# A three-block sequence mixer on one Trainium2 core: parts of VectorE's work handed to ScalarE, GpSimd and TensorE, taps interleaved, and a new hop list

## The chip, the core and the metric

The kernel runs on one NeuronCore of one Trainium2 chip. The metric is the device time of one execution in microseconds (us), as the median of several runs. Engine names as in the profile: PE is TensorE (PEld its weight loads), DVE is VectorE, ACT is ScalarE, POOL is GpSimd, SP is SyncE, whose queue issues all DMAs here.

## The reference, cut to what matters

The input x is 16 batches of 256 tokens with 128 channels, all float32. Four residual blocks follow one another, each on a layer norm of x: a log-linear state-space attention (32 heads of 64), a transformer layer with 16-head attention and 8 experts (top 2), a gated mix of nine shifted copies, and the transformer layer again with the same weights.

```
xBC = sum(xp[:, i:i+T, :] * conv_w[:, i] for i in range(4));  xBC = silu(xBC)      # taps, edge, silu
x, Bm, Cm = split(xBC);  dt, lam = softplus(...), softplus(...)                      # gates
qk = einsum('btgn,bsgn->bgts', Cm, Bm)                                               # qk
att = qk * decay * lam_ts                                                            # weigh, wexp, prod
y = einsum('bhts,bshp->bthp', att, v) + x * D                                        # own, sum
out = x + (y * silu(z) normalised) @ out_proj_w.T + out_proj_b                       # gated, ssq, outp
probs = softmax(q k^T * scale);  out = probs @ v                                     # es, exps, ep, tail 0
h = relu(x @ W1[e] + b1[e]);  ff += w[e] * (h @ W2[e] + b2[e])                       # up, relu, down, acc
```

## The kernel before, in words

The work of one batch is cut into some 290 small steps called hops (`gates` 0 to 6, `conv`/`tap`/`taps`/`silu`/`xt`/`xcopy` 0 to 8, `weigh`/`wexp`/`prod`/`own`/`sum`/`gated` 0 to 7, `smax`/`rowmax`, `es`/`exps`/`ep`, `tail`, `up`/`relu`/`down`/`acc` 0 to 7, `mix` and so on). The string PERIOD is the list of all hops in one turn, written out by hand or by a planner, and "+2" behind a hop means that it works on the batch of two turns ago. `order()` repeats the list for 16 batches plus the largest lag, so in the middle of the run every turn does one whole batch of work, spread over parts of five batches. Each engine walks the same list in order and does its own part of each hop. An engine therefore never overtakes: a wait in one hop holds all its later hops.

The eight PSUM banks form two rings of four (psA for the state-space block, psB for the rest), handed out in list order. PE may run ahead of the engines that empty the banks only by these four.

The parts that the change touches, with the lines of the profile:

- `taps` (L1132): the causal convolution of two channel tiles, three multiply-adds each on DVE from PSUM. Each add waits for the one before it on the same tile, and one tile is done after the other. L1141 then corrects the first three columns of both tiles (the edge), which releases `silu` on ACT (L888).
- `qk` (PE L589, DVE L1145 to L1156): three 128x128 products of B and C. DVE copies them to SBUF, multiplies two of them with the identity and sums rows to get the diagonal, and makes `ccoef`, for which `own` on POOL (L1433) waits.
- `prod` (DVE L1164): the product of the decay weights with QK, for each of eight units one 128x1024 tile on the diagonal, and for the last four units another one off the diagonal, so 12 per batch.
- `gates` 3 and 4 (DVE L1060, L1062, L1065, L1070): pieces of softplus on 128x640.
- `ep` (DVE L1223): copies the attention's sums from PSUM, eight of 128x256 per batch.
- `tail` 0 (DVE L1232, L1234): reciprocal and scaling for each half of the tokens in turn.
- Setup on POOL (L1349 to L1365): fills of the level buffers, q_stack, k_stack and V9, all ahead of batch 0's `gates` 6 (L1370 to L1376), whose result is stored to DRAM (L499) and read back (L508). ACT's first `tap` (L884) waits for that store.

In the list, DVE's longest dense stretch is this one (cut; hops of the kernel before):

```
taps0.3+0 lvl0.3+0 down0.5+2 xcopy0.0+0 xcopy0.1+0 relu0.6+2 up0.7+2 acc0.3+2 zgate0.1+0 taps0.4+0 ...
mix1.2+2 mix1.3+2 tail1.5+3 tail1.6+3 mix1.4+2 mix1.5+2 up1.0+3 relu1.0+3 up1.1+3 ... taps0.8+0
```

Of the kernel before, what the change touches and what calls it, by code (L numbers as in the profile page):

```python
# [108 lines left out]
gates0.2+0 own0.2+1 q1.1+3 sum0.2+1 gated0.1+1 gated0.2+1 own0.3+1 ep0.3+2 weigh0.4+1 tail0.0+2 down1.4+4
weigh0.5+1 acc1.4+4 wexp0.4+1 prod0.4+1 sum0.3+1 wexp0.5+1 up1.6+4 prod0.5+1 own0.4+1 relu1.6+4 gates0.3+0  # L110
sum0.4+1 own0.5+1 gated0.3+1 sum0.5+1 weigh0.6+1 gated0.4+1 gated0.5+1 own0.6+1 own0.7+1 wexp0.6+1 down1.5+4
weigh0.7+1 wexp0.7+1 prod0.6+1 acc1.5+4 smax1.0+3 prod0.7+1 rowmax1.0+3 sum0.6+1 gated0.6+1 sum0.7+1 gated0.7+1
tail0.1+2 smax1.1+3 rowmax1.1+3 tail0.2+2 ssq0.0+1 smax1.2+3 rowmax1.2+3 tail0.3+2 ssq0.1+1 ssq0.2+1 ssq0.3+1
smax1.3+3 outp0.0+1 rowmax1.3+3 maxt1.0+3 down1.6+4 gates0.4+0 outp0.1+1 tail0.4+2 acc1.6+4 gates0.5+0
gates0.6+0 v1.0+3 outp0.2+1 es1.0+3 exps1.0+3 place0.0+0 fn0.0+1 tail0.5+2 conv0.0+0 up0.0+2 ep1.0+3 es1.1+3
relu0.0+2 up1.7+4 exps1.1+3 relu1.7+4 conv0.1+0 fn0.1+1 tap0.0+0 tail0.6+2 ep1.1+3 experts0.0+2 lvl0.0+0 es1.2+3
exps1.2+3 q0.0+1 taps0.0+0 down1.7+4 acc1.7+4 experts1.2+4 experts0.1+2 ep1.2+3 up0.1+2 tap0.1+0 es1.3+3
conv0.2+0 down0.0+2 up0.2+2 zgate0.0+0 up0.3+2 relu0.1+2 down0.1+2 exps1.3+3 tap0.2+0 taps0.1+0 relu0.2+2
down0.2+2 silu0.0+0 acc0.0+2 silu0.1+0 conv0.3+0 zact0.0+0 xt0.0+0 relu0.3+2 tap0.3+0 q0.1+1 lvl0.1+0 up0.4+2
taps0.2+0 down0.3+2 silu0.2+0 relu0.4+2 conv0.4+0 experts1.3+4 acc0.1+2 up0.5+2 xt0.1+0 tap0.4+0 up0.6+2  # L120
relu0.5+2 down0.4+2 acc0.2+2 conv0.5+0 lvl0.2+0 taps0.3+0 lvl0.3+0 down0.5+2 xcopy0.0+0 xcopy0.1+0 relu0.6+2
up0.7+2 acc0.3+2 zgate0.1+0 taps0.4+0 tap0.5+0 acc0.4+2 relu0.7+2 acc0.5+2 down0.6+2 down0.7+2 taps0.5+0
silu0.3+0 acc0.6+2 silu0.4+0 acc0.7+2 xt0.2+0 ep1.3+3 zact0.1+0 experts0.2+2 xcopy0.2+0 conv0.6+0 tap0.6+0
lvl0.4+0 lvl0.5+0 xt0.3+0 conv0.7+0 tap0.7+0 taps0.6+0 tail1.0+3 experts0.3+2 xcopy0.3+0 taps0.7+0 tail1.1+3
lvl0.6+0 silu0.5+0 lvl0.7+0 tail1.2+3 silu0.6+0 xt0.4+0 zgate0.2+0 smax0.0+1 zgate0.3+0 xt0.5+0 mix1.0+2
smax0.1+1 tail1.3+3 silu0.7+0 rowmax0.0+1 conv0.8+0 xcopy0.4+0 zact0.2+0 zact0.3+0 mix1.1+2 tail1.4+3 smax0.2+1
# [58 lines left out]
def build(nc, d, out):  # L185
# [15 lines left out]
    with ctx:  # L201
# [1281 lines left out]
```

## Time and profile before

| | |
|---|---|
| median of 3 runs | 2415.92 us (2415.37 to 2418.28) |
| the profiled execution's own time | 2413.47 us |
| its span in the trace | 2411.6 us |
| mean granted PE clock | 0.97 of full speed |
| busy: PE, PEld, DVE, ACT, POOL | 2117.2, 1603.1, 1880.2, 1411.4, 825.8 us |
| chain that ended last | PE 55%, DVE 27%, issue 6%, POOL 5%, ACT 4%, DMA 2% |

The profiled execution took 1.9 us more than its span, and 2.4 us less than the median of the runs. Busy time says how long an engine had an instruction in work; PE's matmuls overlap, so busy PE is not PE at its peak. The chain is the sequence of work followed back from the last instruction, at each step to what released it.

### The profile page before, as it was taken

The numbers are of one execution on the slowest core, as the hardware profiler recorded it, in microseconds if no ns is written. First come the engines' busy times: TensorE is split into PE (matmuls) and PEld (weight loads), VectorE is DVE, ScalarE is ACT, GpSimd is POOL, SyncE is SP. The second block draws the span as 40 slices with busy tenths as digits, with TensorE's granted clock in tenths as the row PEclk, the third lists the DMA queues.
The fourth block names the chain that finished last, engine by engine and source line by source line (L and its number), as shares of the span: only waits on it lengthen the run. The fifth ranks groups of instructions, "written<-read, shape, count | busy, mean of one in ns | idle before, by whom it ended". The sixth has DMA issues, their size and how long they took to land.

```text
span 2411.6 us, 47467 instructions
## 1 busy us (share of the span) xinstructions
PE 2117.2 (88%) x16768; PEld 1603.1 (66%) x16768; DVE 1880.2 (78%) x4629; ACT 1411.4 (59%) x2980; POOL 825.8 (34%) x1188
## 2 busy tenths in 40 slices
PE   2768889998999899998989999898989999898866
PEld 1546657676777677676767767677767767676544
DVE  7776878788897878788887878888787878865433
ACT  1545556666575766656576666657576665654323
POOL 5111343424333342424333342433334242424131
PEclk9989999999999999999999999999999999998868
DMA  4020212120111212110211212011121211011110
GB/s 144 6 48 6 52 41 50 43 47 19 43 42 41 55 41 50 36 38 29 47 48 41 51 44 46 20 40 45 41 54 41 50 36 38 26 41 45 40 40 5
DMA packets 255194, 100.58 MB, mean 42 GB/s; under 512 B 118552, under 2 KB 253856, under 8 KB 254400
## 3 DMA queue, kind: packets, MB, share of 16 engines
q1 hardware_dynamic: 254960, 97.55, 15.6%
q8 instruction: 136, 2.23, 0.4%
q14 instruction: 98, 0.80, 0.1%
HBM read 51.12 MB, written 46.14 MB: 40 GB/s over the span
## 4 chain that ended last, share of the span: by engine, by line
PE 55%; DVE 27%; issue 6%; POOL 5%; ACT 4%; DMA 2%; SPq 0%; DVEq 0%; POOLq 0%; ACTq 0%
PE psB L810 9%; PE psB L800 8%; DVE work L1132 7%; PE psA L581 5%; PE psB L741 5%; DVE nmax L1212 5%; PE psA L641 4%; DVE att L1164 3%; PE psA L666 3%; PE psA L617 2%; PE psB L726 2%; PE psA L621 2%; POOL O_sb L1417 2%; PE psA L634 2%; PE psB L688 1%
## 5 line engine op out<-in xcount | busy, mean ns | idle before, releaser
L1132 DVE SCALAR_TENSOR_TENSOR work<-psA,c_conv_w,work 128x255 f32<-128x255 f32 (+2 forms) x864 | 401.8, 479 | 42.7 <-ACT work L884 21.6
L581 PE MATMUL psA<-xnT_a,c_w_in 128*128 128x256 f32 x1088 | 310.9, 406 | 37.8 <-DVE work L1132 33.8
L1212 DVE TENSOR_REDUCE nmax<-psB 128x2 f32<-128x512 f32 x512 | 315.5, 677 | 28.0 <-PE psB L708 28.0
L957 ACT ACTIVATE pt<-psB 128x512 f32<-128x512 f32 x512 | 264.3, 603 | 63.8 <-PE psB L727 63.6
L800 PE MATMUL psB<-x1T,c_w 128*128 128x256 f32 x1024 | 275.7, 394 | 21.2 <-ACT hid L999 19.6
L810 PE MATMUL psB<-c_w,hid 128*128 128x128 f32 x2048 | 269.5, 279 | 1.5 <-ACT hid L980 0.8
L810 PEld LDWEIGHTS psB<-c_w,hid 128*128 128x128 f32 x2048 | 259.8, 195 | 15.3 <-issue 5.0
L911 ACT ACTIVATE att<-psA 128x512 f32<-128x512 f32 x384 | 207.5, 604 | 103.6 <-PE psA L617 59.8
L1164 DVE TENSOR_TENSOR att<-att,QK 128x1024 f32<-128x1024 f32 x192 | 253.1, 1352 | 6.0 <-ACT att L911 5.7
L581 PEld LDWEIGHTS psA<-xnT_a,c_w_in 128*128 128x128 f32 x1088 | 197.3, 200 | 85.9 <-DVE work L1132 52.0
L980 ACT ACTIVATE hid<-psB,c_b 128x256 f32<-128x256 f32 x512 | 215.4, 479 | 66.5 <-PE psB L800 51.6
L1289 DVE SCALAR_TENSOR_TENSOR ff<-psB,w_e,ff 128x128 f32<-128x128 f32 x512 | 155.5, 345 | 92.7 <-PE psB L810 87.2
L800 PEld LDWEIGHTS psB<-x1T,c_w 128*128 128x128 f32 x1024 | 183.8, 194 | 63.1 <-ACT hid L999 25.4
L1344 POOL TENSOR_SCALAR var_eps<-lnmv 128x2 f32<-128x2 f32 x128 | 28.9, 226 | 559.8 <-DVE lnmv L1018 558.5
L1433 POOL TENSOR_TENSOR own<-X,ccoef 128x512 f32<-128x512 f32 x128 | 150.5, 1187 | 185.5 <-PE psA L641 92.4
L884 ACT ACTIVATE work<-psA,conv_b,c_conv_w 128x256 f32<-128x256 f32 x288 | 150.4, 572 | 86.1 <-PE psA L581 56.2
L641 PE MATMUL psA<-att,X 128*64 128x128 f32 x3072 | 195.9, 277 | 0.0
L641 PEld LDWEIGHTS psA<-att,X 128*64 128x64 f32 x3072 | 165.1, 137 | 21.4 <-issue 21.4
L1385 POOL CAST qparts<-qkf 128x256 bf16<-128x256 f32 x64 | 35.5, 555 | 390.7 <-ACT qkf L943 387.0
L706 PE MATMUL psB<-k_stack,q_stack 72*128 72x256 bf16 x512 | 136.0, 291 | 32.2 <-issue 17.5
L1417 POOL TENSOR_TENSOR O_sb<-O_sb,hid 128x256 f32<-128x256 f32 x128 | 101.6, 794 | 135.3 <-DVE hid L1314 126.0
L741 PE MATMUL psB<-pt,V 128*32 128x256 f32 x2048 | 137.0, 385 | 7.7 <-ACT pt L957 7.6
(234 smaller groups left out, 4309.9 us busy)
## 6 DMA issues: line engine op xcount, KB each, us to landing
qk_scr<-qparts SPq DMA_DIRECT2D x192, 192.0 KB, 2.3
q_stack<-qk_scr SPq DMA_DIRECT2D x32, 576.0 KB
k_stack<-qk_scr SPq DMA_DIRECT2D x32, 576.0 KB
lvl_scr<-work SPq DMA_DIRECT2D x32, 192.0 KB, 5.4
low<-lvl_scr SPq DMA_DIRECT2D x256, 1.5 KB
c_w_in<-in_in_wT SPq DMA_DIRECT2D x1, 2176.0 KB, 8.5
x<-in_x SPq DMA_DIRECT2D x16, 128.0 KB, 2.2
c_w<-in_W SPq DMA_DIRECT2D x2, 1024.0 KB
```

The source lines that it names most:

```text
L581: e.matmul(t[:, 0:T], w_in[:, first + j * P:first + (j + 1) * P], xnT_a[:, :], start=True, stop=True).then_inc(filled[b], 1)
L641: m = e.matmul(t[j * HD:(j + 1) * HD, f * P:(f + 1) * P], X[:, s, fc + j * HD:fc + (j + 1) * HD], att[:, 2 * f + j, :], start=False, stop= ...
L741: m = e.matmul(t[32 * j:32 * j + 32, 0:T], V9[:, kt, 4 * g + j, :], pt[:, j % 2, :], start=(kt == 0), stop=(kt == NT - 1), skip_group_chec ...
L800: e.matmul(t[:, 0:T], w_1[:, k, j * P:(j + 1) * P], x1T_b[lay][:, :], start=True, stop=True).then_inc(filled[b], 1)
L810: m = e.matmul(t[:, i * P:(i + 1) * P], hb[:, j, i * P:(i + 1) * P], w_2[:, 2 * k + j, :], start=(j == 0), stop=(j == 1))
L911: e.activation(att[:, :, c:c + 64], t[:, :].rearrange("p (t h) -> p h t", h=HG), ACT.Exp).then_inc(drained[b], 1)
L957: e.activation(pt_b[a % PTS][:, :, :].rearrange("p h q -> p (h q)"), t[:, :], ACT.Exp, scale=float(AD) ** -0.5).then_inc(drained[b], 1)
L980: e.activation(hid_b[lay][k % 2][:, j, :], t[:, 0:T], ACT.Relu, bias=b_1[:, 2 * k + j:2 * k + j + 1]).then_inc(drained[b], 1)
L1132: m = e.scalar_tensor_tensor(out=cv[:, back:], in0=t[:, 0:T - back], scalar=conv_w[:, c, tap:tap + 1], in1=cv[:, back:], op0=ALU.mult, op1 ...
L1164: e.tensor_tensor(att[:, :, :], att[:, :, :], bc(QK[:, kq, :], 1, HG), ALU.mult).then_inc(att_done, 1)
L1212: e.tensor_reduce(nmax[:, i, 2 * h2:2 * h2 + 2], t[:, :].rearrange("p (h k) -> p h k", k=T), AX.X, ALU.max).then_inc(drained[b], 1)
L1289: m = e.scalar_tensor_tensor(out=ff[:, i, :], in0=t[:, i * P:(i + 1) * P], scalar=w_e[:, i, k:k + 1], in1=ff[:, i, :], op0=ALU.mult, op1=A ...
```

## The change

The hop list PERIOD is new. It has 316 hops instead of 292, its first hop is at another place of the turn, and six names are new: `edge` (8 steps, POOL, and one for k = 0), `bcp` (POOL), `qkc` (ACT), `coef` (DVE), `ocopy` (8, ACT) and `prodp` (4, POOL). DVE's dense stretch now reads (cut):

```
taps0.4+1 acc0.5+3 silu0.3+1 ocopy1.3+4 taps0.5+1 xcopy0.1+1 zgate0.1+1 edge0.4+1 silu0.4+1 acc0.6+3 ...
mix1.4+3 mix1.5+3 mix1.6+3 conv0.8+1 mix1.7+3 experts1.0+4 up1.1+4 tap0.8+1 lvl0.7+1 xcopy0.6+1 ... mix1.8+3
```

and the one with the products (cut):

```
weigh0.4+1 wexp0.4+1 up1.5+4 up1.6+4 own0.4+1 weigh0.5+1 prodp0.4+1 acc1.3+4 gated0.1+1 relu1.5+4 prod0.3+1
ep0.3+2 gated0.2+1 gates0.3+0 down1.4+4 prod0.4+1 sum0.3+1 wexp0.5+1 sum0.4+1 ...
```

PE, in `qk` and `sum` (`bc_prod` is B times C, made on POOL; its column sums are the diagonal):

```diff
+                    e.wait_ge(bc_product, n + 1)
+                    for i in range(NT):
+                        m = e.matmul(t[:, 3 * P + i:3 * P + i + 1], bc_prod[:, i * P:(i + 1) * P], ones_f[:, 0:1],
+                                     start=True, stop=True, skip_group_check=True)
...
-                    e.wait_ge(att_done, 12 * n + tile_index(0, tt, hg, tt) + 1)
+                    e.wait_ge(att_done, NU * n + k + 1)
+                    if tt:
+                        e.wait_ge(att_done_pool, H // HG * (n - 1) + k + 1)
```

ACT (new hops):

```diff
+                elif what == "qkc":
+                    e.activation(QK_all[:, :], t[:, 0:3 * P + NT], ACT.Copy).then_inc(drained[b], 1)
+                elif what == "ocopy":
+                    e.activation(O_sb[:, k, :], t[:, 0:T], ACT.Copy).then_inc(drained[b], 1)
```

DVE: `qk`'s copy and diagonal and `ep`'s copy are gone, `coef` keeps the rest of `qk`, `prod` keeps the diagonal tile of each unit, and:

```diff
-                    e.wait_ge(w_ready, n + 1)
-                    e.scalar_tensor_tensor(out=W1t[:, :, :], in0=W2t[:, :, :], scalar=-1.0, in1=W1t[:, :, :],
-                                           op0=ALU.add, op1=ALU.subtract).then_inc(*own.step())
-                    e.scalar_tensor_tensor(out=U[:, :, :], in0=U[:, :, :], scalar=0.0, in1=W1t[:, :, :],
-                                           op0=ALU.max, op1=ALU.subtract).then_inc(*own.step())
+                    e.tensor_scalar(U[:, :, :], U[:, :, :], 0.0, None, ALU.max).then_inc(u_ready, 1)
...
-                    e.tensor_tensor(SPL[:, :, :], SPL[:, :, :], U[:, :, :], ALU.add).then_inc(*own.step())
+                    e.wait_ge(spl_ready, n + 1)
...
+                    for back in range(1, KCONV):
+                        for j, c in enumerate(conv_tiles(k)):
+                            if back == 1:
+                                e.wait_ge(tap_done, tap_count(n, c))
+                            else:
+                                e.wait_ge(dve_step, done[j])
                             m = e.scalar_tensor_tensor(out=cv[:, back:], in0=t[:, 0:T - back], ...
...
+                    for qt in range(NT):
+                        e.wait_ge(*full(hop, qt))
+                        e.reciprocal(rden[:, qt, :], heads[qt][:, :, AD]).then_inc(*own.step())
+                    for qt in range(NT):
+                        e.wait_ge(dve_step, own.n - NT + 1 + qt)
+                        e.tensor_tensor(o_tok[:, qt, :]..., bc(rden[:, qt, :], 2, AD), ALU.mult)
```

POOL (new work; the fills of q_stack, k_stack and V9 and four of the eight fills of `low_buf` move behind batch 0's `gates` 6, the other four to `gates` 5):

```diff
+                elif what == "gates" and k == 3:
+                    e.tensor_scalar(w_less[:, :, :], W2t[:, :, :], 1.0, None, ALU.subtract).then_inc(*own.step())
+                    e.tensor_tensor(W1t[:, :, :], w_less[:, :, :], W1t[:, :, :], ALU.subtract).then_inc(*own.step())
+                    e.wait_ge(u_ready, n + 1)
+                    e.tensor_tensor(U[:, :, :], U[:, :, :], W1t[:, :, :], ALU.subtract).then_inc(*own.step())
+                    e.wait_ge(ln_ready, n + 1)
+                    e.tensor_tensor(SPL[:, :, :], SPL[:, :, :], U[:, :, :], ALU.add).then_inc(spl_ready, 1)
+                elif what == "bcp":
+                    e.tensor_tensor(bc_prod[:, :], bmT, cmT, ALU.mult).then_inc(bc_product, 1)
+                elif what == "edge":
+                    e.tensor_tensor(edge, edge, conv_edge[:, first:first + 2, :], ALU.add).then_inc(conv_done, 1)
+                elif what == "prodp":
+                    e.tensor_tensor(att[:, :, :], att[:, :, :], bc(QK[:, 2, :], 1, HG), ALU.mult).then_inc(att_done_pool, 1)
```

Besides, `lvl_scale` lies in the buffer X instead of one of its own, and `rden` has a row for each token half.

## Rows read from the trace of the kernel before

**Rows 1.** The page, part 1: busy us (share of the span), instructions.
```profile
PE 2117.2 (88%) x16768; PEld 1603.1 (66%) x16768; DVE 1880.2 (78%) x4629; ACT 1411.4 (59%) x2980; POOL 825.8 (34%) x1188
```

**Rows 2.** The chain that ended last, in time: start, length, what.
```profile
497.56 3.57 PE psA L666 x32
...
1876.20 3.57 PE psA L666 x32
```

**Rows 3.** Windows, one turn: length, busy (x) by engine, PE clock, DMA.
```profile
911.30:1049.20 137.90, 127.79 (x1050) 97.94 (x1049) 115.53 (x288) 87.57 (x186) 49.76 (x73) 1.00 0.16 42
```

**Rows 4.** Windows, four stretches of the next turn, same columns.
```profile
1060.00:1096.90 36.90, 35.71 (x265) 28.65 (x265) 31.29 (x98) 29.14 (x65) 11.26 (x20) 1.00 0.35 80
1096.90:1129.00 32.10, 25.32 (x144) 18.19 (x143) 29.08 (x80) 19.48 (x45) 13.66 (x21) 1.00 0.04 11
1129.00:1159.70 30.70, 30.49 (x272) 22.17 (x271) 19.31 (x52) 23.88 (x50) 13.32 (x21) 1.00 0.15 40
1159.70:1171.80 12.10, 10.54 (x116) 7.93 (x114) 11.80 (x15) 4.65 (x10) 6.76 (x6) 1.00 0.31 99
```

**Rows 5.** Groups by line: xcount | busy us, mean ns | idle before, releaser.
```profile
L1223 DVE COPY O_sb<-psB 128x256 f32<-128x256 f32 x128 | 54.1, 423 | 113.6 <-PE psB L741 113.5
...
L1387 POOL TENSOR_TENSOR qkf<-qkf,qparts 128x256 f32<-128x256 f32 x64 | 43.1, 673 | 5.2
...
L1141 DVE TENSOR_TENSOR work<-work,conv_edge 128x6 f32<-128x6 f32 x144 | 27.5, 191 | 15.4 <-DVE work L1132 0.5
...
L1060 DVE TENSOR_SCALAR work<-work 128x640 f32<-128x640 f32 x16 | 20.1, 1254 | 1.6 <-ACT work L864 1.6
L1372 POOL TENSOR_TENSOR work<-work 128x512 f32<-128x512 f32 x16 | 19.8, 1241 | 1.3
...
L1148 DVE TENSOR_TENSOR qk_scr<-QK,c_ident 128x128 f32<-128x128 f32 x32 | 15.0, 470 | 1.1
...
L1062 DVE SCALAR_TENSOR_TENSOR work<-work 128x640 f32<-128x640 f32 x16 | 14.6, 915 | 0.6
...
L1065 DVE SCALAR_TENSOR_TENSOR work<-work 128x640 f32<-128x640 f32 x16 | 13.9, 869 | 0.6
L1070 DVE TENSOR_TENSOR SPL<-SPL,work 128x640 f32<-128x640 f32 x16 | 13.7, 858 | 0.4 <-issue 0.3
...
L935 ACT ACTIVATE srcT<-psB 128x256 f32<-128x256 f32 x32 | 12.4, 386 | 32.1 <-PE psB L682 32.1
...
L1150 DVE TENSOR_REDUCE qk_diag<-qk_scr 128x1 f32<-128x128 f32 x32 | 9.2, 286 | 1.1
...
L1145 DVE COPY QK<-psA 128x384 f32<-128x384 f32 x16 | 8.8, 550 | 6.5 <-PE psA L589 6.5
...
L673 PE MATMUL psA<-share,att 128*128 128x1 f32 x32 | 4.5, 210 | 0.0
```

**Rows 6.** The chain inside the dense stretch, from one turn.
```profile
1097.97 0.49 DVE work L1132
1098.49 0.88 DVE work L1132 x2
```

**Rows 7.** Tiles att on DVE and own on POOL, one turn: ns min/median/max.
```profile
L1164 DVE TENSOR_TENSOR att<-att,QK x12: 1210/1218/2059, 1136.7 to 1176.5; 128x1024 f32<-128x1024 f32 x12
...
L1433 POOL TENSOR_TENSOR own<-X,ccoef x8: 1044/1046/1856, 1135.3 to 1170.3; 128x512 f32<-128x512 f32 x8
```

**Rows 8.** Timeline of DVE in the stretch from 1159.7 us.
```profile
1161.29 6.27 DVE L1164 TENSOR_TENSOR att<-att,QK 128x1024 f32<-128x1024 f32 x4
```

**Rows 9.** Timeline of the start: POOL fills, first store, first tap.
```profile
18.84 10.33 POOL L1355 CAST low<-c_ident 32x1024 bf16<-32x1024 f32 x8
...
36.28 3.50 POOL L1361 MEMSET k_stack<- 32x4096 bf16 x1
...
44.99 2.06 SPq L499 DMA_DIRECT2D lvl_scr<-work  x2
...
51.06 1.93 ACT L884 ACTIVATE work<-psA,conv_b,c_conv_w 128x256 f32<-128x256 f32 x4 [23.68 <-DMA lvl_scr<-work]
```

More of the change, by code:

```diff
@@ L109 @@
[L109 to L113, printed above, removed]
@@ L1124, in _ @@
                 elif what == "taps":
-                    pair = conv_pair(k - 1)
-                    for j, c in enumerate(conv_tiles(k)):
-                        t, b, u = bank(("conv", 0, n, k), j)
-                        cv = pair[:, j, :]
-                        e.wait_ge(tap_done, tap_count(n, c))
-                        for back in range(1, KCONV):
-                            tap = KCONV - 1 - back
+                    done = [0, 0]
+                    for back in range(1, KCONV):
+                        tap = KCONV - 1 - back
+                        for j, c in enumerate(conv_tiles(k)):
+                            t, b, u = bank(("conv", 0, n, k), j)
+                            cv = conv_pair(k - 1)[:, j, :]
+                            if back == 1:
+                                e.wait_ge(tap_done, tap_count(n, c))
+                            else:
+                                e.wait_ge(dve_step, done[j])
                             m = e.scalar_tensor_tensor(out=cv[:, back:], in0=t[:, 0:T - back], scalar=conv_w[:, c, tap:tap + 1],
@@ L1135, in _ @@
                                 m.then_inc(*own.step())
-                                e.wait_ge(*own.now())
-                        m.then_inc(drained[b], 1)
-                    edge = pair[:, :, 0:KCONV - 1]
-                    e.wait_ge(*empty(("conv", 0, n, k), 0))
-                    e.wait_ge(*empty(("conv", 0, n, k), 1))
-                    e.tensor_tensor(edge, edge, conv_edge[:, conv_tiles(k)[0]:conv_tiles(k)[0] + 2, :], ALU.add).then_inc(conv_done, 1)
-                elif what == "qk":
-                    t, b, u = bank(hop)
-                    e.wait_ge(filled[b], u + 1)
-                    e.tensor_copy(QK[:, :, :].rearrange("p k t -> p (k t)"), t[:, 0:3 * P]).then_inc(drained[b], 1)
-                    e.wait_ge(*empty(hop))
-                    for i in range(NT):
-                        e.tensor_tensor(qk_scr[:, :], QK[:, i, :], ident[:, :], ALU.mult).then_inc(*own.step())
-                        e.wait_ge(*own.now())
-                        e.tensor_reduce(qk_diag[:, i:i + 1], qk_scr[:, :], AX.X, ALU.add).then_inc(*own.step())
-                        e.wait_ge(*own.now())
+                                done[j] = own.n
+                            else:
+                                m.then_inc(drained[b], 1)
+                elif what == "coef":
+                    e.wait_ge(*empty(("qk", 0, n, 0)))
                     for i in range(NT):
@@ L1158, in _ @@
                     tt, hg = UNITS[k]
[L1159 to L1164 removed]
+                    att = att_b[tile_index(n, tt, hg, tt) % ATTS]
+                    e.wait_ge(*empty(("qk", 0, n, 0)))
+                    e.wait_ge(*empty(("weigh", 0, n, k), 2 * tt))
+                    e.wait_ge(*empty(("weigh", 0, n, k), 2 * tt + 1))
+                    e.tensor_tensor(att[:, :, :], att[:, :, :], bc(QK[:, tt, :], 1, HG), ALU.mult).then_inc(att_done, 1)
                 elif what == "gated":
```

142 lines of the change are left out of this document (79 added, 63 removed).

## The prediction, made before the changed kernel had run

> **What bounds the kernel now.** I read the page first. PE has the most busy time, 88% of the span, and DVE is at 78% [rows 1]. An average over unlike stretches does not say which of them the time hangs on, so I went on to the turns. In the chain of waits the 32 matmuls of `outp` (L666) mark each turn. Ten turns lie between 497.56 and 1876.20, so a turn takes 137.86 us [rows 2]. In one turn PE is busy for 127.8 us and DVE for 115.5 us, and ACT and POOL are far below [rows 3]. The PE clock is granted in full there, so the clock is not what is at stake.
>
> Then I cut one turn where the chain changes engines [rows 4]. The reader is to see two kinds of stretch. From 1060 to 1096.9 and from 1129 to 1159.7 PE is busy almost without a gap (35.7 of 36.9 us and 30.5 of 30.7 us). From 1096.9 to 1129 DVE is busy for 29.1 of 32.1 us while PE falls to 25.3, and from 1159.7 to 1171.8 DVE has 11.8 of 12.1 us. PE's and DVE's totals are close, but their loads come at different times, and four banks of PSUM don't carry one over to the other. The turn costs what PE needs in its stretches plus what DVE needs in its own. **DVE's work counts only in its own stretches**, some 44 us of a turn. Taking it away under a full PE saves nothing.
>
> **The change part by part, per turn.** Group totals divided by 16 batches.
>
> *Copies of the attention's sums.* DVE loses 54.1 us in all, 3.4 per turn [rows 5]. None of it is in a DVE stretch: DVE waits for PE before most of these copies (113.6 us in all). ACT gets eight copies of 128x256 from PSUM. The same shape takes 386 ns there [rows 5], so 3.1 us on an engine that is busy for 87.6 of 137.9. Cost and gain nothing. Without ACT's spare time each would put 0.4 us before the next exponential.
>
> *Copy of QK and the diagonal.* DVE loses (8.8 + 15.0 + 9.2)/16 = 2.1 us [rows 5], under PE's stretch, so nothing on the path. POOL gets one 128x256 product (0.67 us, L1387) and PE two 128x1 matmuls, each two instructions in float32. The nearest row is L673 with 0.21 us each, so 0.84 us if nothing overlaps; from below, a quarter of that as other matmuls overlap. It lies in a PE stretch: plus 0.2 to 0.9, I take **plus 0.5**.
>
> *Edges.* Nine per turn at 191 ns. DVE loses 1.7 us, of which the three or four in the dense stretch count: **minus 0.6**. POOL's price for 128x6 is not in the trace. From above it is L1387's 0.67 us for 256 columns, from below nothing. I take 0.3. `silu` then waits for a hand-over to another engine's queue. What hides it is that `silu` stands several hops behind `edge` in the list for most pairs; with that cover gone each costs its 0.3 us and the hand-over.
>
> *Taps in turn.* Six adds now take about 2.94 us: in the chain one that waits for its predecessor costs 0.49 plus a gap of 0.03, while two with no wait between them take 0.88 together [rows 6], so 0.40 for the second. With two tiles in turn every add has another one between it and its predecessor: 6 x 0.40 = 2.4 at best, 2.94 at worst. I take 0.45 us off each of the nine, 4.0 per turn, three of them in the dense stretch: **minus 1.3**. `tail` 0 gets the same trick for **minus 0.1**.
>
> *Products.* Four of 12 go to POOL, 4 x 1.218 = 4.9 us of DVE [rows 7]. In the second DVE stretch four products stand in a row and take 6.27 us, not 4.9 [rows 8], since `own` runs on POOL beside them. Two of these go: **minus 2.7**, and the others lie where PE is nearly full, minus 0.3. POOL's price for 128x1024 is not in the trace. Its 512 columns take 1.046 us undisturbed [rows 7] and 1.241 in another place (L1372), and 256 columns 0.673. The two slopes give 1.8 and 2.4 us, so 7 to 10 us of POOL per turn. I take 2.0 each. PE's `sum` now waits for POOL too, and all of PE's later hops behind it. Before, a unit's two products took 2.4 us one after the other on DVE, so a POOL product of 2.0 beside one of DVE's comes no later, if POOL is free when it is due.
>
> *Softplus pieces.* DVE loses (14.6 + 13.9 + 13.7)/16 = 2.6 us and gets one 128x640 scalar operation, whose twin L1060 averages 1.25 us [rows 5]: net minus 1.4, of which I count **minus 0.4** in the second stretch. POOL gets four operations of 128x640, by L1372 some 1.5 us each, 6 us. `gates` 4 waits for the last one, some 50 hops later in the list, which hides it; if not, the level store is late.
>
> *The new list.* I counted the hops in DVE's dense stretch. Before, from `taps` 3 to `taps` 8, it holds six `taps`, five `acc` and three `rowmax`. In the new list, from `taps` 4 to `mix` 8, it holds five `taps`, three `acc`, three `rowmax`, and three more `mix` steps and a `v`; on PE three `down` are gone and three `mix` matmuls added. A `taps` is 2.9 us, and the small ones nearly cancel, so DVE's excess over PE there falls by 1 to 2 us beyond edges and interleaving. But what left the stretch stands elsewhere: `taps` 0 to 3 and `gates` 6 now crowd behind `outp`. I count **minus 0.5**, between nothing and minus 4.
>
> *Against it:* POOL grows from 50 to about 70 us per turn, and I charge **plus 0.5** for DVE operations that it slows.
>
> Sum: +0.5 -0.6 -1.4 -3.0 -0.4 -0.5 +0.5 = -4.9, say 5.0 us per turn. The run has 20 turns, of which 13 are full and four at the ends partly so. I count 15.5: **minus 78 us**.
>
> *Start.* POOL fills the low buffer from 18.84 us on for 10.3 us, then the stacks and V9 (the third of those fills still starts at 36.28), all before `gates` 6. The store goes out at 44.99, and the first `tap` follows at 51.06 after 23.7 us of waiting [rows 9]. With the stacks' fills, over 11 us, behind the store and four steps of softplus (6 us) in front of it, the store goes out 5 to 10 us sooner. I take **minus 8**. It could be nothing if the read-back of levels ends last.
>
> Against the profiled execution's 2413.5 us: 2413.5 - 78 - 8 = 2327.5. The median of the runs is 2.4 us above that execution, so **2330 us**.
>
> **The port, row and rule.** L1164 has a median of 1218 ns and a longest of 2059, L1433 1046 and 1856, where the two overlap [rows 7, 8]: the loser gains almost the other's whole length (0.84 of 1.05 us). The Trainium skill, page "SBUF — State Buffer", section "SBUF: two separate sides", says that an operation of VectorE with two SBUF inputs and one of GpSimd take the shared port pair as an exclusive lock, so that the second "fully blocks". By that rule a product given to POOL is not taken from DVE's time wherever DVE has a product of its own to do. The trace agrees. The second rival below is made of this, from the rows.
>
> **Rivals.**
>
> 1. *The new list closes nearly all gaps of PE.* PE is idle for 10 us per turn [rows 3]. If all of it goes, 10 x 15.5 + 8 = 163 us and the time is about 2253. For it: DVE falls to some 98 us per turn and could follow everywhere. Against it: the dense stretch still has twice as much DVE as PE work.
>
> 2. *POOL's operations block DVE's* (the slower side). The place is `prodp` and `gates` 3 beside `prod`, from `weigh` 4 to `sum` 7. Price: 0.8 of the POOL operation as in the rows above, 4 x 0.8 x 2.2 = 7 us for the products and 1 for the softplus pieces, so 8.0 instead of the 0.5 charged. Net +2.5 per turn, +39 - 8, **about 2447**. It decides from 5.5 us of blocked time per turn on. Against it: between `sum` 0 and `weigh` 5 the new list gives DVE little beyond three products and three `gated`, so that it has room to be blocked in.
>
> 3. *The saved work was hidden anyway, or a hand-over takes its place.* `edge` stands in POOL's queue behind affine steps, roots and mix sums, each of which waits for another engine. Nine hand-overs of 0.3 us plus a queue wait of the same size are 5 us per turn, as much as the gain: about 2410, from 2400 to 2425.
>
> **How the numbers follow.** My forecast gets 0.53, rival 1 0.20, rival 2 0.15, rival 3 0.12. Its own bounds: with the taps at 2.94, no contention relief and no early store it is 1.5 us per turn, 2390; with the list's 4 us and PE's matmuls at 0.2 it is 9 us per turn, 2268. The range reaches from rival 1 nearly to the middle of rival 3, 2255 to 2412. What a measurement of this kernel can tell from no change is about 0.2%, 5 us. Faster by more: forecast, rival 1 and a third of rival 3, 0.77. Within: 0.05. Slower: 0.18.
>
> **What would show it.** Right: turns of about 133 us; DVE near 98 us per turn; six adds in about 2.5 us; no DVE wait for a `prodp`; the store at 35 to 40 us. Wrong towards rival 1: turns under 129 us with PE gaps gone. Rival 2: L1164's median near 2 us and PE waiting for L1164 or `prodp`. Rival 3: ACT's L888 waiting for POOL and PE for `silu`. The prediction fails if the turn is not shorter by 2 to 9 us.

## The result and the profile after

The changed kernel takes 2471.3 us (median of 4 runs, 2468.06 to 2477.97). The kernel before took 2415.64 beside it. The ratio is 1.0233 with a 95% interval of 1.0208 to 1.0259, so the change is **slower by 2.3%**, where 3.6% faster was forecast.

The page of the changed kernel, its first part and the clock line:

```profile
PE 2158.8 (87%) x16832; PEld 1655.1 (67%) x16832; DVE 1695.3 (69%) x4181; ACT 1456.1 (59%) x3124; POOL 1168.5 (47%) x1476
...
PEclk9999989999999999999999999999999999998876
```

The hand-over of work is there as planned: DVE lost 185 us of busy time against [rows 1], and POOL gained 343. None of it reached the end time. PE's busy time rose from 2117.2 to 2158.8 us and its mean granted clock fell from 0.97 to 0.94: of the 60.4 us by which the span is longer, 41.6 are busy PE and 18.8 idle PE (span less busy time). The 64 instructions that PE gained in `qk` are not the reason, since the run below with the products back has them too, and a busy PE of 2118.1. Now the turns, first in the chain that ended last (start, length, what), then as a window like [rows 3]:

```profile
513.16 3.57 PE psA L679 x32
...
2193.13 3.57 PE psA L679 x32
```

```profile
1074.90:1215.00 140.10, 129.54 (x1054) 101.00 (x1053) 103.28 (x260) 90.11 (x195) 71.62 (x91) 0.98 0.17 41
```

Twelve turns lie between the two marks: 140.0 us each. The same twelve turns of the kernel before end at 2148.59, and with [rows 2] that is 137.6 each. So 29 us of the 60 us of longer span come from the turns. The rest lies at the ends: the first mark stands 15.6 us later than the one in [rows 2], and after the last one the changed kernel needs 278.9 us where the kernel before needed 263.0.

**Where a turn loses it.** The chain inside the turn from 1074.9, the stretch in which `gates` 3 and 4 stand between the products:

```profile
1178.76 1.70 issue
1180.48 2.36 POOL att L1409
1182.92 2.68 POOL work L1358
1185.68 1.55 POOL work L1360
1187.31 1.55 POOL work L1363
1188.95 2.56 POOL SPL L1366
1191.53 1.05 DVE work L1085
1192.58 0.98 DVE work L1086
...
1195.01 2.37 DVE work L1088
1197.38 0.13 DVE gc L1092
```

The chain lies on POOL for 11 us: the product L1409, then the four softplus pieces, which the forecast had called covered. DVE waits for the last (L1085), and the products and `gated` steps behind it wait in DVE's queue. The next view, the timeline of three engines in the same place (start, length, engine, line, what, in brackets the idle time before), shows what else is odd:

```profile
1191.46 1.04 POOL L1466 TENSOR_TENSOR own<-X,ccoef 128x512 f32<-128x512 f32 x1
1192.46 4.84 POOL L1409 TENSOR_TENSOR att<-att,QK 128x1024 f32<-128x1024 f32 x2
```

```profile
1191.53 1.05 DVE L1085 TENSOR_TENSOR work<-SPL,c_neg_a 128x64 f32<-128x64 f32 x1 [1.43 <-POOL SPL L1366]
1192.50 2.59 DVE L1086 TENSOR_SCALAR work<-SPL 128x512 f32<-128x512 f32 x1
1195.01 2.37 DVE L1088 SCALAR_TENSOR_TENSOR work<-SPL 128x64 f32<-128x64 f32 x1
```

```profile
1192.63 0.41 PE L567 MATMUL psA<-work,c_tri 128*128 128x32 f32 x2 [2.09 <-DVE work L1085]
...
1194.95 1.09 PE L647 MATMUL psA<-c_ident,own 128*128 128x128 f32 x4 [0.56 <-POOL att L1409]
1195.97 2.88 PE L654 MATMUL psA<-att,X 128*64 128x128 f32 x32
...
1201.73 0.39 PE L628 MATMUL psA<-high,high_sel 117*128 117x512 bf16 x1 [1.90 <-DVE Z L1176]
...
1204.21 1.97 PE L654 MATMUL psA<-att,X 128*64 128x128 f32 x32
```

DVE's L1085 and L1088 have 64 columns each and two inputs in SBUF. They take 1.05 and 2.37 us, and each ends when the POOL operation beside it ends (1.04 and 2.42 us long). By the Trainium skill's page "SBUF — State Buffer", section "SBUF: two separate sides", the later of the two "fully blocks"; the trace agrees. L1086 between them has a single input, and it too takes 2.59 us, until POOL's first product ends. These three steps of `gates` 4 are where DVE is slowed most. Over the whole run, first of the kernel before (mean ns behind the comma), then of the changed one:

```profile
L1073 DVE TENSOR_SCALAR work<-SPL 128x512 f32<-128x512 f32 x16 | 7.6, 472 | 0.0
...
L1072 DVE TENSOR_TENSOR work<-SPL,c_neg_a 128x64 f32<-128x64 f32 x16 | 4.3, 269 | 0.5
...
L1075 DVE SCALAR_TENSOR_TENSOR work<-SPL 128x64 f32<-128x64 f32 x16 | 4.3, 269 | 0.0
```

```profile
L1086 DVE TENSOR_SCALAR work<-SPL 128x512 f32<-128x512 f32 x16 | 40.1, 2504 | 0.0
...
L1088 DVE SCALAR_TENSOR_TENSOR work<-SPL 128x64 f32<-128x64 f32 x16 | 36.6, 2289 | 0.0
...
L1085 DVE TENSOR_TENSOR work<-SPL,c_neg_a 128x64 f32<-128x64 f32 x16 | 16.7, 1047 | 26.5 <-POOL SPL L1366 26.5
```

L1073 has become L1086, L1072 L1085 and L1075 L1088. The three cost 1.0 us per turn before and 5.8 now. PE waits three times between 1190.5 and 1201.7, and its clock falls. The windows (length, PE, PEld, DVE, ACT, POOL busy, granted clock):

```profile
1192.00:1194.00 2.00, 1.37 (x12) 1.37 (x13) 2.00 (x2) 0.00 (x0) 2.00 (x2) 1.00 0.00 0
1194.00:1196.00 2.00, 1.44 (x10) 0.90 (x8) 2.00 (x2) 0.63 (x1) 2.00 (x2) 0.62 0.00 0
1196.00:1198.00 2.00, 2.00 (x21) 2.00 (x22) 2.00 (x4) 0.26 (x1) 2.00 (x2) 0.53 0.00 0
```

From 1194 to 1198 PE is granted 0.62 and 0.53, near the lower of its two levels (1.2 and 2.4 GHz), after the gap of 2.09 us in front of L567. The 32 matmuls of L654 took 2.88 us there and 1.97 at 1204.2, so this gap cost nearly a microsecond on these matmuls alone, on top of its own length. The turn's mean clock is 0.98 where [rows 3] has 1.00.

### The profile page after: what moved, and what is told of

Read it like the earlier page. It is cut to its first block, busy times and chain, and to the rows that moved or that the text cites. A ratio compares the mean times of both kernels' runs of the same rounds, so it can differ in the third digit from the quotient of the medians.

```text
span 2472.0 us, 47645 instructions
## 1 busy us (share of the span) xinstructions
PE 2158.8 (87%) x16832; PEld 1655.1 (67%) x16832; DVE 1695.3 (69%) x4181; ACT 1456.1 (59%) x3124; POOL 1168.5 (47%) x1476
## 4 chain that ended last, share of the span: by engine, by line
PE 53%; DVE 22%; POOL 13%; issue 6%; ACT 4%; DMA 1%; SPq 0%; POOLq 0%; DVEq 0%; ACTq 0%
PE psB L823 7%; PE psB L813 7%; PE psA L588 5%; DVE nmax L1216 5%; DVE work L1148 5%; PE psA L654 5%; PE psA L679 5%; PE psB L754 4%; PE psB L842 2%; PE psB L739 2%; PE psA L647 2%; POOL att L1409 2%; PE psB L719 2%; POOL work L1358 2%; PE psB L740 2%
## 5 line engine op out<-in xcount | busy, mean ns | idle before, releaser
L1148 DVE SCALAR_TENSOR_TENSOR work<-psA,c_conv_w,work 128x255 f32<-128x255 f32 (+2 forms) x864 | 348.5, 473 | 26.9 <-ACT work L897 26.8
L588 PE MATMUL psA<-xnT_a,c_w_in 128*128 128x256 f32 x1088 | 290.1, 390 | 21.7 <-DVE work L1148 12.7
L823 PE MATMUL psB<-c_w,hid 128*128 128x128 f32 x2048 | 275.3, 281 | 6.4 <-ACT pt L978 3.4
L978 ACT ACTIVATE pt<-psB 128x512 f32<-128x512 f32 x512 | 264.0, 603 | 19.9 <-PE psB L740 18.8
L588 PEld LDWEIGHTS psA<-xnT_a,c_w_in 128*128 128x128 f32 x1088 | 192.2, 193 | 61.0 <-DVE work L1148 27.9
L1168 DVE TENSOR_TENSOR att<-att,QK 128x1024 f32<-128x1024 f32 x128 | 199.5, 1578 | 43.4 <-ACT att L932 41.9
L654 PE MATMUL psA<-att,X 128*64 128x128 f32 x3072 | 213.2, 292 | 0.0
L654 PEld LDWEIGHTS psA<-att,X 128*64 128x64 f32 x3072 | 181.7, 147 | 24.4 <-issue 24.4
L1466 POOL TENSOR_TENSOR own<-X,ccoef 128x512 f32<-128x512 f32 x128 | 167.8, 1317 | 54.2 <-PE psA L654 51.4
L1409 POOL TENSOR_TENSOR att<-att,QK 128x1024 f32<-128x1024 f32 x64 | 157.1, 2463 | 31.8 <-ACT att L932 27.1
L628 PE MATMUL psA<-high,high_sel 117*128 117x512 bf16 x384 | 127.9, 386 | 20.3 <-DVE Z L1176 17.7
```

The costliest lines, as they stand in the source:

```text
L588: e.matmul(t[:, 0:T], w_in[:, first + j * P:first + (j + 1) * P], xnT_a[:, :], start=True, stop=True).then_inc(filled[b], 1)
L654: m = e.matmul(t[j * HD:(j + 1) * HD, f * P:(f + 1) * P], X[:, s, fc + j * HD:fc + (j + 1) * HD], att[:, 2 * f + j, :], start=False, stop= ...
L823: m = e.matmul(t[:, i * P:(i + 1) * P], hb[:, j, i * P:(i + 1) * P], w_2[:, 2 * k + j, :], start=(j == 0), stop=(j == 1))
L978: e.activation(pt_b[a % PTS][:, :, :].rearrange("p h q -> p (h q)"), t[:, :], ACT.Exp, scale=float(AD) ** -0.5).then_inc(drained[b], 1)
L1148: m = e.scalar_tensor_tensor(out=cv[:, back:], in0=t[:, 0:T - back], scalar=conv_w[:, c, tap:tap + 1], in1=cv[:, back:], op0=ALU.mult, op1 ...
L1168: e.tensor_tensor(att[:, :, :], att[:, :, :], bc(QK[:, tt, :], 1, HG), ALU.mult).then_inc(att_done, 1)
```

## The experiments

All changes are against the changed kernel unless the old list is named; every ratio is to the kernel before, run beside it. The runs are told by what they settle.

**Which edit, in the new list: softplus.** The four pieces go back to VectorE:

```diff
-                elif what == "gates" and k == 3:
-                    e.tensor_scalar(w_less[:, :, :], W2t[:, :, :], 1.0, None, ALU.subtract).then_inc(*own.step())
...
+                    e.scalar_tensor_tensor(out=W1t[:, :, :], in0=W2t[:, :, :], scalar=-1.0, in1=W1t[:, :, :],
+                                           op0=ALU.add, op1=ALU.subtract).then_inc(*own.step())
...
+                    e.scalar_tensor_tensor(out=U[:, :, :], in0=U[:, :, :], scalar=0.0, in1=W1t[:, :, :],
+                                           op0=ALU.max, op1=ALU.subtract).then_inc(*own.step())
...
+                    e.tensor_tensor(SPL[:, :, :], SPL[:, :, :], U[:, :, :], ALU.add).then_inc(*own.step())
```

> The changed kernel with the four softplus pieces back on VectorE, list and all else as changed. Theory A (a relay through GpSimd: in each turn VectorE and then TensorE wait for 8.6 us of softplus pieces that stand in GpSimd's queue behind a product): TensorE's wait before the cumulative sums, 47 us in all, goes, and with it most of the 8 to 10 us that a turn loses there: 135 us per turn or less, 2360 to 2400. Theory B (the new list itself costs the time, whatever engine does the pieces): little changes, 2450 to 2480. Theory C (the port: GpSimd's products slow VectorE's): 2440 to 2470, since the products stay where they are.

Measured: 2451.1 us, ratio 1.0138 (1.0117 to 1.0160). The relay costs 20 us, not the 70 to 110 that theory A asked for. PE's wait for DVE's operand of the cumulative sums (L567) didn't go; it rose from 47 to 66 us, with the products still on GpSimd. Theory A falls as the main cause; 2451 lies in the ranges of both B and C.

**Products.** They go back to DVE in `prod`, the off-diagonal one first, and `prodp` does nothing:

```diff
-                elif what == "prodp":
...
+                    if tt:
+                        att = att_b[tile_index(n, tt, hg, 0) % ATTS]
...
+                        e.tensor_tensor(att[:, :, :], att[:, :, :], bc(QK[:, 2, :], 1, HG), ALU.mult).then_inc(att_done_pool, 1)
```

> The changed kernel with the off-diagonal products back on VectorE, all else as changed. Theory A: GpSimd's softplus pieces start up to 2.4 us sooner, but the relay stays: 2430 to 2470. Theory B: 2450 to 2490. Theory C: VectorE's product falls from a mean of 1578 ns to about 1300 and the time to 2400 or less.

Measured: 2412.2 us, ratio 0.9979 (0.9960 to 0.9998). **59 us, the whole loss, goes with this one step.** The groups of tile att, first of the changed kernel, then of this run (count, busy us, mean ns, idle before):

```profile
L1168 DVE TENSOR_TENSOR att<-att,QK 128x1024 f32<-128x1024 f32 x128 | 199.5, 1578 | 43.4 <-ACT att L932 41.9 <-DVE ff L1234 0.2
...
L1409 POOL TENSOR_TENSOR att<-att,QK 128x1024 f32<-128x1024 f32 x64 | 157.1, 2463 | 31.8 <-ACT att L932 27.1 <-issue 4.5
```

```profile
L1173 DVE TENSOR_TENSOR att<-att,QK 128x1024 f32<-128x1024 f32 x128 | 187.6, 1484 | 7.8 <-ACT att L932 7.8
...
L1169 DVE TENSOR_TENSOR att<-att,QK 128x1024 f32<-128x1024 f32 x64 | 85.2, 1332 | 19.1 <-ACT att L932 17.8
```

Theory C comes nearest, but neither of its numbers came: its product was to fall to about 1300 ns (1484 and 1332; `own` and the softplus pieces still run beside it), and the time to 2400 or less. The products are also not where most of DVE's lost time was. The steps of `gates` 4 in this run:

```profile
L1086 DVE TENSOR_SCALAR work<-SPL 128x512 f32<-128x512 f32 x16 | 8.3, 521 | 0.0
...
L1088 DVE SCALAR_TENSOR_TENSOR work<-SPL 128x64 f32<-128x64 f32 x16 | 4.2, 264 | 0.0
```

With L1085 (16.7 to 5.9 us) they give DVE 75 us back in all, while the 128 diagonal products give 12. PE is busy for 2118.1 us of a span of 2410.1: of the 61.9 us by which the span is shorter than the changed kernel's, 40.7 are busy PE, at a mean clock of 0.96 instead of 0.94, and 21.2 idle PE.

**Everything back, in the new list; and every edit, in the old list.** These two part the list from the edits. In the second, each new hop stands directly behind the one it came from, `prodp` in front of `prod`.

> The new list with every hand-over undone: softplus pieces, products, edges, attention copies and the diagonal on VectorE, taps one tile after the other. It tells what the list alone does. Theory A: the list is sound by itself, 2400 to 2430, about the kernel before. Theory B: the list is the loss, 2460 or more. Theory C: as A.

> The old list with every edit of the change, each new hop directly behind (products on GpSimd: in front of) the one that it was part of. It tells what the edits alone do. Theory A: the relay stands in the old list too, 2400 to 2470. Theory B: the edits alone are faster than the kernel before, 2330 to 2380. Theory C: 2420 to 2460, with products near 1600 ns.

Measured: 2602.4 us, ratio 1.0764 (1.0747 to 1.0780), and 2665.3 us, ratio 1.1022 (1.1006 to 1.1038). The second lies outside every range. The first lies in theory B's (2460 or more), but B blamed the list whatever engine does the work, and the same list with only the products back takes 2412.2. The new list without the edits loses 184 us, the edits without the new list lose 247, both together lose 56. **List and assignment hold only as a pair.** A hop's worth is not a property of the hop.

**Length of POOL's queue or the port?** POOL's product is replaced by fills of the same tile, which read no tensor. The off-diagonal products are left out of the result in both runs.

```diff
-                    e.tensor_tensor(att[:, :, :], att[:, :, :], bc(QK[:, 2, :], 1, HG), ALU.mult).then_inc(att_done_pool, 1)
+                    e.memset(att[:, :, :], 0.0).then_inc(*own.step())
+                    e.wait_ge(*own.now())
+                    e.memset(att[:, :, :], 0.0).then_inc(att_done_pool, 1)
```

> The changed kernel with GpSimd's product replaced by two fills of the same tile, some 2.2 us, which read nothing (the off-diagonal products are left out of the result). GpSimd's queue is as long as before. If the port is the cost of the products (GpSimd and VectorE both reading SBUF twice): VectorE's products fall from a mean of 1578 to about 1300 ns and the time to 2420 or less, as with the products on VectorE. If it is the length of GpSimd's queue, ahead of softplus pieces and own: 2455 to 2475.

The second run has one more `e.memset(att[:, :, :], 0.0)` with its wait.

> As the run with two fills in place of GpSimd's product, but with three: two took 1.9 us, less than the product's 2.46, three take 2.9, more than it (off-diagonal products left out of the result again). If GpSimd's reading of SBUF is what costs (the port): still 2425 or less, 45 us under the changed kernel. If the length of GpSimd's queue is: 2470 or more.

Measured: two fills 2412.7 us, ratio 0.9987 (0.9976 to 0.9998); three fills 2449.7 us, ratio 1.0136 (1.0123 to 1.0150). Groups of the run with two fills, with two of the steps of `gates` 4:

```profile
L1168 DVE TENSOR_TENSOR att<-att,QK 128x1024 f32<-128x1024 f32 x128 | 174.2, 1379 | 46.2 <-ACT att L932 44.6 <-DVE ff L1234 0.3
...
L1411 POOL MEMSET att<- 128x1024 f32 x64 | 63.6, 994 | 3.7
...
L1409 POOL MEMSET att<- 128x1024 f32 x64 | 61.0, 953 | 28.8 <-ACT att L932 27.3 <-issue 1.4
...
L1086 DVE TENSOR_SCALAR work<-SPL 128x512 f32<-128x512 f32 x16 | 18.8, 1173 | 0.0
...
L1088 DVE SCALAR_TENSOR_TENSOR work<-SPL 128x64 f32<-128x64 f32 x16 | 4.1, 257 | 0.0
```

Two fills are 1.95 us, three (955, 952 and 994 ns) 2.90, and the third costs 1.49% for its 0.95 us. The firm part first: three fills hold POOL's queue longer than a product of 2.46 us, and yet the run is 0.97%, some 23 us, faster than the changed kernel. At least that much comes with what the product reads. For the rest an estimate: 2.46 us lies 0.54 of the way from two fills to three, and by length alone, if it counts evenly (not shown), the ratio would be 1.0067. It is 1.0233. So roughly 1.7%, 40 us, comes with the reading, and the rest of the step's cost with length. What the reading slows is DVE's L1088 (2289 ns against 257), L1086 (2504 against 1173) and the products (1578 against 1379 to 1434). The fills are not free of blocking either: L1086, with its single input, takes 1173 ns beside them and 472 in the kernel before, so 40 us may be too low. The run with three fills alone would have misled: 2450 lies between what the two theories said, and both hold in part.

**The same move in the old list**, with the taps in turn as its base. Both runs have this list (cut); in the base no engine does anything at `prodp`, and the run moves the product to GpSimd there:

```
... own0.2+1 ... weigh0.4+1 ... wexp0.4+1 prodp0.4+1 prod0.4+1 sum0.3+1 wexp0.5+1 up1.6+4 prodp0.5+1 prod0.5+1 own0.4+1 ...
```

```diff
-                    if tt:
...
-                        e.tensor_tensor(att[:, :, :], att[:, :, :], bc(QK[:, 2, :], 1, HG), ALU.mult).then_inc(att_done_pool, 1)
...
+                elif what == "prodp":
...
+                    e.tensor_tensor(att[:, :, :], att[:, :, :], bc(QK[:, 2, :], 1, HG), ALU.mult).then_inc(att_done_pool, 1)
```

In the base, softplus pieces, products, edges, copies and diagonal are all on VectorE; the setup order and the two-step reciprocal are the changed kernel's.

> The old list with only the taps in turn, the two-step reciprocal and the new order of setup; all work that moved engines is back on VectorE. By the forecast's terms (1.4 us per turn over 15.5 turns and 8 us at the start): 2380 to 2395. If the list is what holds the turn: 2405 to 2420.

> The old list with taps in turn (2406 us) and the off-diagonal products on GpSimd, each directly in front of VectorE's. The forecast gave this move 3 us per turn, some 46 us: 2360. If the port gives VectorE nothing and the sums wait for GpSimd's 2.4 us: 2440 to 2520, and the move is the wrong step whatever the list.

Measured: the base 2406.2 us, ratio 0.9959 (0.9943 to 0.9974), the best of all runs; with the products on GpSimd 2508.6 us, ratio 1.0376 (1.0361 to 1.0391). The base's groups, then those with the move:

```profile
L1185 DVE TENSOR_TENSOR att<-att,QK 128x1024 f32<-128x1024 f32 x128 | 157.4, 1239 | 3.3 <-ACT att L920 3.3
...
L1181 DVE TENSOR_TENSOR att<-att,QK 128x1024 f32<-128x1024 f32 x64 | 101.0, 1577 | 2.6 <-ACT att L920 1.9 <-issue 0.4
```

```profile
L1180 DVE TENSOR_TENSOR att<-att,QK 128x1024 f32<-128x1024 f32 x128 | 260.5, 2046 | 37.6 <-ACT att L920 37.1
...
L1403 POOL TENSOR_TENSOR att<-att,QK 128x1024 f32<-128x1024 f32 x64 | 181.5, 2856 | 17.3 <-ACT att L920 17.2
```

This is the plainest reading of the study. VectorE needs 258.4 us for all 192 products, and 260.5 for 128 of them when GpSimd does the other 64. A third of the work moved and none of DVE's time did. GpSimd spent 181.5 us, and in this run PE waits 70.3 us for `own` (L1460) behind the products in GpSimd's queue.

**The start, and the taps.** This run takes the taps' interleaving out of the base:

```diff
-                    for back in range(1, KCONV):
-                        for j, c in enumerate(conv_tiles(k)):
+                    for j, c in enumerate(conv_tiles(k)):
+                        for back in range(1, KCONV):
...
+                                e.wait_ge(*own.now())
```

> The old list, taps one tile after the other again; left of the change are the new order of setup, the moved constant and the two-step reciprocal. By the forecast (8 us at the start): 2405 to 2412. If the early store buys nothing, because later work is not ready for it: 2413 to 2418, and the 9 us of the run with taps in turn are the taps'.

Measured: 2413.0 us, ratio 0.9975 (0.9963 to 0.9986). So the setup, with the two-step reciprocal that this run keeps, is worth about 6 us where 8 were forecast for the start alone, and the taps in turn only 0.16% more, 4 us, with intervals that overlap (0.9943 to 0.9974 with them). The group of the taps in the changed kernel, to compare with 401.8 us and 479 ns before:

```profile
L1148 DVE SCALAR_TENSOR_TENSOR work<-psA,c_conv_w,work 128x255 f32<-128x255 f32 (+2 forms) x864 | 348.5, 473 | 26.9 <-ACT work L897 26.8
```

348.5 us over 864 is 0.403 us each, as read from [rows 6]. The adds before were a little cheaper than the chain showed (401.8 us over 864 is 0.465, not 0.49), so DVE lost 3.3 us per turn to the forecast's 4.0. In the old list this hardly came off the turn. In the new list it does count:

> The changed kernel with products on VectorE (2412 us) and the taps one tile after the other. In the old list the taps in turn were worth at most 9 us of the forecast's 20. If the same here: 2418 to 2428. If the new list, made for faster taps, falls out of step without them: 2440 or more.

Measured: 2460.7 us, ratio 1.0183 (1.0162 to 1.0203), 49 us slower than with the taps in turn, as the second of the two readings said.

**The other moves, one at a time, in either list.** Each puts one operation on the other engine, softplus as in the diff above, and:

```diff
-                elif what == "edge":
+                    e.tensor_tensor(edge, edge, conv_edge[:, first:first + 2, :], ALU.add).then_inc(conv_done, 1)
...
-                    e.activation(O_sb[:, k, :], t[:, 0:T], ACT.Copy).then_inc(drained[b], 1)
+                    e.tensor_copy(O_sb[:, k, :], t[:, 0:T]).then_inc(drained[b], 1)
...
-                elif what == "bcp":
+                        e.tensor_tensor(bc_prod[:, 0:P], QK[:, i, :], ident[:, :], ALU.mult).then_inc(*own.step())
+                        e.tensor_reduce(qk_diag[:, i:i + 1], bc_prod[:, 0:P], AX.X, ALU.add).then_inc(*own.step())
```

These lines take the edges, the copies and the diagonal back to VectorE; the runs with a move lack them. The three runs in the new list stand on the one with the products back (0.9979), the four in the old list on the base (0.9959).

> Products and softplus pieces back on VectorE, list as changed. If the two costs are separate (59 and 20 us so far): 2385 to 2400, faster than the kernel before. If the softplus pieces cost only because they stood behind the products: 2405 to 2430, VectorE now pays 1.4 us more per turn.

> Products and the copies of the attention's sums back on VectorE, at the place in the list where ScalarE had them. The forecast counted this move at nothing, because VectorE does it under TensorE's stretch: 2405 to 2420. If in the new list a copy at its place holds VectorE until TensorE's sums are there, and the PSUM ring behind it: 2450 to 2500, and it is a large part of the 190 us between the new list with and without the hand-overs.

> The changed kernel with products and edges back on VectorE. VectorE pays nine times some 0.2 us per turn, GpSimd's queue no longer stands between taps and silu. If the hand-over costs as much as it saves: 2405 to 2420, as without it (2412). If the edges in the dense stretch count as forecast (0.6 us per turn): 2420 to 2430. If silu waits for GpSimd: 2380 to 2400.

> The old list with taps in turn (2406 us) and the softplus pieces on GpSimd. By the forecast (0.4 us per turn): 2395 to 2405. If VectorE, which waits for the last piece in order, passes the wait on: 2420 to 2480.

> The old list with taps in turn (2406 us) and the edges on GpSimd, each directly behind its taps. By the forecast (0.6 us per turn): 2393 to 2403. If silu waits in GpSimd's queue: 2410 to 2440.

> The old list with taps in turn (2406 us) and the copies of the attention's sums on ScalarE. If VectorE's waits for these sums (7 us per turn) hold it back before its dense stretch: 2380 to 2400, the best so far. If they lie under TensorE's stretch, as the forecast says: 2400 to 2412.

> The old list with taps in turn (2406 us) and the diagonal made by GpSimd, TensorE and ScalarE. By the forecast (0.5 us per turn more on TensorE): 2410 to 2418. If VectorE's shorter way to the first own counts (about 2 us per turn, in front of the first sum): 2385 to 2400. If the copy on ScalarE holds its exponentials in this list: 2420 or more.

| what the other engine takes | old list: ratio with it (without 0.9959) | new list: ratio without it (with 0.9979) |
|---|---|---|
| softplus pieces, GpSimd | 1.0495 (1.0476 to 1.0514) | 1.0057 (1.0034 to 1.0080) |
| edges, GpSimd | 1.0113 (1.0096 to 1.0131) | 1.0094 (1.0078 to 1.0110) |
| attention copies, ScalarE | 1.0106 (1.0085 to 1.0127) | 1.0192 (1.0174 to 1.0210) |
| diagonal, GpSimd, TensorE and ScalarE | 0.9982 (0.9971 to 0.9992) | not tried |

Of these seven runs four fell outside every range given for them: softplus (2538.8), edges (2446.5) and copies (2441.8) in the old list, and the edges back in the new one (2437.8). The expectations read single edits no better than the forecast did. The pattern is the same three times (the diagonal, alone in the old list, lost 0.2% with intervals that touch): handing the step over loses in the old list, and taking it back loses in the new one. Only the products lose in both. The worth also hangs on the other moves: with the products still on GpSimd, taking softplus back gained 20 us in the same new list. The largest entry is the softplus relay in the old list, +132 us, from 2406.2 to 2538.8, a step that the forecast had booked as a small gain. For the copies in the new list the trace shows where a part of the loss comes: with them back on VectorE, PE waits 26.3 us in all for DVE's copy in front of L739.

**A try at the best of both.** In the changed kernel GpSimd's first softplus piece (L1358) takes 2.59 us, and DVE's scalar operation of the same shape (L1082) 0.67. With the products on VectorE, the base of this run, the piece takes 2.03.

```profile
L1358 POOL TENSOR_SCALAR work<-work 128x640 f32<-128x640 f32 x16 | 41.4, 2588 | 1.7 <-DVE work L1081 0.4
...
L1082 DVE TENSOR_SCALAR work<-work 128x640 f32<-128x640 f32 x16 | 10.7, 669 | 0.0
```

```diff
+                    e.tensor_scalar(w_less[:, :, :], W2t[:, :, :], 1.0, None, ALU.subtract).then_inc(u_ready, 1)
...
-                    e.tensor_scalar(w_less[:, :, :], W2t[:, :, :], 1.0, None, ALU.subtract).then_inc(*own.step())
```

> The changed kernel with products on VectorE (2412 us), and of GpSimd's four softplus pieces the first, a scalar subtraction of 2.7 us, on VectorE, where the like takes 0.5 us. If the relay of softplus pieces is what VectorE and TensorE still wait for (38 us of TensorE's waits): 2385 to 2402, faster than the kernel before and than any run so far. If the waits are set by the place of the step in the list: 2405 to 2415.

Measured: 2411.6 us, ratio 0.9981 (0.9969 to 0.9993), the same as without it. The relay became shorter (6.3 us for its three pieces, where the four took 7.8), PE's wait for L567's operand fell only from 38 to 32 us, and the time stayed. This fits the second reading, that the step's place in the list sets the wait; no run moved the step to show it. Of all kernels run, the old list with the taps in turn and the new setup is the fastest, 0.41% under the kernel before.

## Why the prediction was wrong

- **The stretches: neither shown nor refuted as a picture, but no basis for a sum.** DVE fell by 185 us and no time was gained, which fits. The copies of the attention's sums, which lie in no stretch of DVE and were therefore booked at nothing, moved the time by 36 and 51 us.
- **Products on GpSimd: the step that failed.** It was booked at minus 3.0 us per turn, with 0.5 against it for slowed DVE operations: some 39 us of gain over 15.5 turns. The runs show plus 59 us in all in the new list and plus 102 in the old. The forecast had read the very rows, 1218 and 2059 ns [rows 7], and took the second from a stretch where `own` lay beside the product. It then charged the lock with 0.5 us per turn, where its own rival had 8. The three steps of `gates` 4 alone took 4.8 us per turn more than before, and no part of the forecast names them. They also account for DVE being busy for 103.3 us in the turn shown, where 98 was forecast. The price of the operation, 2.0 us, was low too: 2.36 at the median, 2.46 on average.
- **Rival 2 was right in kind, not in its working.** It gave 2447 and plus 2.5 us per turn, and the turns are 2.4 longer. Its place (`prodp` and `gates` 3 beside `prod`) is where the chain of the changed kernel lies. It had 0.15. That the turn agrees is in part luck: the other terms of its sum failed too, and its sign didn't show, since the median of the products (now L1168) stayed at 1224 ns. At least half of the products were not slowed, and the small steps of `gates` 4 were. What spoke against it, that DVE had room to be blocked in, didn't help: PE waits 47 us in all for L1085.
- **Softplus: wrong cover.** "Some 50 hops later in the list" counted hops, not time. GpSimd's queue brings the pieces to their end 8.6 us after the product in front of them, and `gates` 4 was due then. Beside the products they cost 20 us; with the products back on VectorE they gain 0.8%, and in the old list they cost 5.4%. The row taken for DVE's scalar operation, L1060 at 1.25 us [rows 5], was itself a slowed one: undisturbed it took 0.49, and the new operation of this shape, L1082, takes 0.67 on average.
- **Copies and edges: right as costs, wrong as gains.** A copy takes 395 ns on ScalarE (386 forecast) and an edge 199 ns on GpSimd (300). But the copies were booked at nothing and the edges at minus 0.6 us per turn, 9 us. In the new list the copies on ScalarE are worth 51 us and the edges 28; in the old one they cost 36 and 37. The forecast took each edit at the old list's place and added the list as a term of minus 0.5 us per turn, between 0 and minus 4. The list decides the sign of three of the moves, and the size of the taps.
- **Taps.** The price per add, 0.40, was right to 1%, and six adds take 2.40 to 2.50 us, as the sign asked. The gain on the path was 4 us in the old list, where 20 was booked, and 49 in the new one.
- **Start.** The store went out at 35.04 us, in the window forecast, and the run with the new setup gains 6 us in the old list. What was left out is that a new list also reshapes the turns that are only partly filled: 31 us at the two ends, and still some 19 us with the products back (first mark 505.62, last 2135.86, span 2410.1).
- **The clock.** "The clock is not what is at stake" held for the kernel before only, and this is the larger half of the account. Of the longer span 41.6 us are busy PE at a lower granted clock (0.94 in the mean against 0.97) and only 18.8 idle PE. Gaps of PE that the change opened brought their own slow matmuls, for which the forecast had no term.
- **Rivals 1 and 3.** PE's gaps did not close: idle PE rose from 294.4 to 313.2 us, so rival 1 falls. Rival 3's sign is there but small: `silu` on ACT (L909) waits 25.2 us in all for GpSimd's edges, and 25.3 in the run with the products back, which loses nothing.

What stays open: how much of the loss the blocked steps would have cost at the full clock, since no run holds the clock still; which pairs of hops in the new list tie the copies and taps to it, and whether a list made for products on VectorE would bring the 135.9 us turn (twelve turns in 1630.2 us) down further or mend the ends. No list was made for it.

## What to carry to other kernels

Before work goes from VectorE to GpSimd, look for what VectorE does at that moment: if both read two operands from SBUF, the work is not shared but queued, and a 64-column step can take 2.4 us. Here even a step with one input was held. Look first at the small steps that PE waits for, not at the largest group. And a gap in TensorE's work is to be charged with the slower matmuls behind it, not with its length alone. In a kernel whose engines walk one fixed list, an edit and its list must be costed and tried together: the same edit, the copies on ScalarE, gained 51 us in one list and lost 36 in the other. And a wait is covered by time on the queue that runs ahead of it, not by a number of list entries.

## What the hardware showed unexpectedly

- GpSimd's scalar operation on 128x640 takes 1.99 us (mean of its group in the run with softplus on GpSimd in the old list), more than its two-tensor operation of the same shape (1.53 there). In the changed kernel it stands beside a product of VectorE and takes 2.59.
- A DVE operation on 64 columns ended with the GpSimd operation beside it, after 1.05 and 2.37 us; taking a third of the products from VectorE left its product time at 260.5 us against 258.4.
- Beside a fill on GpSimd, DVE's step with two inputs was not slowed (L1088, 257 ns against 269 before) and its step with one input was (L1086, 1173 against 472). Beside a product both were (2289 and 2504).
- Two fills of 1.95 us on GpSimd gave the same time as the product on VectorE (2412.7 and 2412.2 us), though VectorE is spared 85 us of products in the run with the fills. A product of 2.46 us in their place cost 59 us.
